# Inverting softmax denominators on 128 partitions by way of a small HBM tensor

## What is computed

```python
dots = jnp.einsum('bhid,bhjd->bhij', q, k) * d ** (-0.5)
dots = jnp.where(mask[None, None], mask_value, dots)
attn = jax.nn.softmax(dots, axis=-1)
out = jnp.einsum('bhij,bhjd->bhid', attn, v)
```

## Time and profile before

| | |
|---|---|
| three runs | 5416.88, 5419.1, 5422.39 us, median 5419.1 |
| profiled execution | span 5418.5 us from first to last instruction; no other time of it is given |
| TensorE (PE) busy | 5303.0 us, 98% |
| VectorE (DVE) busy | 3828.9 us, 71% |
| GpSimd (POOL) busy | 3028.9 us, 56% |
| ScalarE (ACT) busy | 2615.1 us, 48% |
| attention stage | about 727 to 2455 us |

### The profile page before, as it was taken

How to read it: one execution, slowest core, us unless ns; L and a number is a source line. 1 busy time by engine, 2 the same in 40 slices (tenths; PEclk the granted TensorE clock), 3 DMA queues, 4 the chain that set the end, 5 groups by cost and what they waited for, 6 DMA issues and landing times. The chain is left out here.

```text
span 5418.5 us, 102292 instructions
## 1 busy us (share of the span) xinstructions
PE 5303.0 (98%) x32880; PEld 4440.9 (82%) x32880; DVE 3828.9 (71%) x7311; ACT 2615.1 (48%) x3833; POOL 3028.9 (56%) x2716
## 2 busy tenths in 40 slices
PE   8999989999999999998999999999999999999999
PEld 6888866766666667667999999989999999999786
DVE  6666667778787877775676666766667666666664
ACT  3333333333343333335666666666666666666410
POOL 1222215666666665115777777777777777777514
PEclk9999989999999999998999999999999999999999
DMA  7777764444454444435676677767787676676748
GB/s 239 248 242 255 250 173 129 133 134 119 136 148 135 119 141 118 134 98 119 134 158 112 134 170 150 163 132 167 158 227 158 135 164 129 134 156 113 178 154 289
DMA packets 500414, 864.75 MB, mean 160 GB/s; under 512 B 64388, under 2 KB 165493, under 8 KB 497694
## 3 DMA queue, kind: packets, MB, share of 16 engines
q1 hardware_dynamic: 356014, 567.12, 33.2%
q0 software_dynamic: 140928, 292.13, 29.5%
q10 hardware_dynamic: 3312, 3.47, 0.3%
HBM read 498.49 MB, written 330.47 MB: 153 GB/s over the span
## 5 line engine op out<-in xcount | busy, mean ns | idle before, releaser
L1754 POOL DMA_INDIRECT mid_base<-e_rows,e_ox x556 | 1160.3, 2087 | 372.5 <-POOL e_ox L1749 239.5
L1865 DVE TENSOR_TENSOR e_wgu_lo<-e_wgu,e_wgu_hi 128x2048 fp32r<-128x2048 f32 x278 | 637.5, 2293 | 806.4 <-ACT e_wgu_hi L1788 676.6
L1742 POOL DMA_INDIRECT e_xg<-mid_xn,e_ix x556 | 625.5, 1125 | 336.4 <-POOL e_ix L1739 226.4
L1801 ACT CAST e_xT_hi<-e_ps_t 128x512 fp32r<-128x512 f32 x556 | 299.1, 590 | 929.8 <-PE e_ps_t L1931 929.8
L1069 POOL DMA_INDIRECT mid_ids<-b_pairs,b_cell x512 | 614.3, 1200 | 141.8 <-issue 141.0
L1944 PE MATMUL e_ps_g<-e_xT_hi,e_wgu_hi 128*128 128x256 f32 x2224 | 652.9, 294 | 1.7 <-issue 1.7
L1944 PE MATMUL e_ps_g<-e_xT_lo,e_wgu_hi 128*128 128x256 f32 x2224 | 630.0, 283 | 0.0
L1944 PE MATMUL e_ps_g<-e_xT_hi,e_wgu_lo 128*128 128x256 f32 x2224 | 629.7, 283 | 0.0
L1944 PE MATMUL e_ps_u<-e_xT_hi,e_wgu_hi 128*128 128x256 f32 x2224 | 629.4, 283 | 0.0
L1944 PE MATMUL e_ps_u<-e_xT_lo,e_wgu_hi 128*128 128x256 f32 x2224 | 629.4, 283 | 0.0
L1944 PE MATMUL e_ps_u<-e_xT_hi,e_wgu_lo 128*128 128x256 f32 x2224 | 629.4, 283 | 0.0
(11 more groups left out here) (286 smaller groups left out, 13368.0 us busy)
## 6 DMA issues: line engine op xcount, KB each, us to landing
b_xT_hi<-mid_xT_hi SPq DMA_DIRECT2D x32, 1024.0 KB
b_xT_lo<-mid_xT_lo SPq DMA_DIRECT2D x32, 1024.0 KB
mid_base<-b_x SPq DMA_DIRECT2D x32, 1024.0 KB
e_wgu<-in_gate_w SPq DMA_DIRECT2D x62, 512.0 KB
e_wgu<-in_up_w SPq DMA_DIRECT2D x62, 512.0 KB
e_wd<-in_down_w SPq DMA_DIRECT2D x62, 512.0 KB
ec_cell<-mid_base SPq DMA_DIRECT2D x88, 256.0 KB, 4.9
ab_q<-mid_q_hi SPq DMA_DIRECT2D x82, 256.0 KB, 4.0
```

What stands on the lines that cost most here:

```text
L1742: pool.indirect_dma_start(xg[s][:, i, :], None, t["xn"], bass.IndirectOffsetOnAxis(ap=ix[s][:, i:i + 1], axis=0))\
L1754: pool.indirect_dma_start(t[f"base{i}"], bass.IndirectOffsetOnAxis(ap=ox[s][:, i:i + 1], axis=0), rows[s][:, i, :], None, compute_op=ALU.a ...
L1801: act.copy(xT_hi[s][:, i * DC // 2 * RB:(i + 1) * DC // 2 * RB], ps_t[i][:, :]).then_inc(xT_hi_ready, 1)
L1865: dve.tensor_tensor(wgu_lo[s][:, :], wgu[s][:, :], wgu_hi[s][:, :].bitcast(F32), ALU.subtract)\
```

## The change

One of the 32 equal rows of each head's denominators is copied from `den` into a new tile `den16` of 128 partitions and 16 columns (`turn_den`), inverted there in one instruction (`invert`), stored to a new HBM tensor `rden` of 4 x 512 (`store_rden`), and loaded from there so that each of the four rows lands on 32 partitions of a new tile `rden` (`spread_rden`). `finish` multiplies by `rden` and waits for that load. The three transfers are issued by ScalarE, behind the exponents of slots 2, 5 and 7; the reciprocal stands in slot 4 of VectorE. The four reciprocals of 128 columns in slots 2 to 5 go.

```diff
@@ stage_b, tiles and semaphores @@
         den = sb("den", [P, QC])
+        den16 = sb("den16", [P, QC // DH])
+        rden = sb("rden", [P, QC])
...
-        rden_ready = sem("rden_ready")
+        den16_in = sem("den16_in")
+        den16_ready = sem("den16_ready")
+        rden_out = sem("rden_out")
+        rden_in = sem("rden_in")
@@ GpSimd @@
             def finish(u):
-                pool.wait_ge(rden_ready, QTC * (u + 1))
+                pool.wait_ge(rden_in, 16 * (u + 1))
                 pool.wait_ge(od_emptied, u + 1)
                 if u >= 2:
                     pool.wait_ge(att_out[u % 2], 16 * (u // 2))
-                pool.tensor_tensor(att[u % 2][:, :], o[:, :], den[:, :], ALU.mult).then_inc(att_ready, 1)
+                pool.tensor_tensor(att[u % 2][:, :], o[:, :], rden[:, :], ALU.mult).then_inc(att_ready, 1)
@@ ScalarE @@
+            def turn_den(u):
+                act.wait_ge(den_ready, u + 1)
+                act.dma_start(den16[:, :], den[0:P:DH, :].rearrange("h (j c) -> h j c", j=DH)).then_inc(den16_in, 16)
+
+            def store_rden(u):
+                act.wait_ge(den16_ready, u + 1)
+                act.dma_start(t["rden"].rearrange("h (j c) -> (h j) c", j=DH), den16[:, :]).then_inc(rden_out, 16)
+
+            def spread_rden(u):
+                act.wait_ge(rden_out, 16 * (u + 1))
+                if u:
+                    act.wait_ge(att_ready, u)
+                act.dma_start(rden[:, :], t["rden"][:, None, :].broadcast_to([HPC, DH, QC])).then_inc(rden_in, 16)
...
                     for kt, h in t_slots(n, k):
                         exponent(u, kt, h)
+                    if u and k == 2:
+                        turn_den(u - 1)
+                    if u and k == 5:
+                        store_rden(u - 1)
+                    if u and k == 7:
+                        spread_rden(u - 1)
...
+            turn_den(NU - 1)
+            store_rden(NU - 1)
+            spread_rden(NU - 1)
@@ VectorE @@
                 if u:
                     dve.wait_ge(att_ready, u)
+                    dve.wait_ge(den16_in, 16 * u)
                 dve.tensor_tensor(den[:, :], ps_d[:, :], p_null[:, :], ALU.add).then_inc(den_ready, 1)
...
-            def invert(u, i):
-                dve.wait_ge(den_ready, u + 1)
-                part = den[:, i * P:(i + 1) * P]
-                dve.reciprocal(part, part).then_inc(rden_ready, 1)
+            def invert(u):
+                dve.wait_ge(den16_in, 16 * (u + 1))
+                dve.reciprocal(den16[:, :], den16[:, :]).then_inc(den16_ready, 1)
...
-                    if 2 <= k < QTC + 2 and u:
-                        invert(u - 1, k - 2)
+                    if k == 4 and u:
+                        invert(u - 1)
...
-            for i in range(QTC):
-                invert(NU - 1, i)
+            invert(NU - 1)
@@ tensors in HBM @@
+        rden=d("rden", (HPC, QC))
```

More of the change, by code:

```diff
@@ L2322, in internal @@
         cnt=d("cnt", (P, EXPERTS)), ids=d("ids", (NSLOT, 2), I32), blk=d("blk", (1, 3 * P), I32), used=d("used", (1, 3), I32),
-        attT=d("attT", (DC, P, TOK)), passed=nc.alloc_semaphore("passed"))
+        attT=d("attT", (DC, P, TOK)), rden=d("rden", (HPC, QC)), passed=nc.alloc_semaphore("passed"))
 def layout(L0_attn_x, L0_attn_Wqkv, L0_attn_conv_w, L0_attn_conv_b, L0_attn_null_k, L0_attn_null_v, L0_attn_W_out,
```

## The result

The changed kernel takes 5638.71 us in the median, the kernel before 5417.99 in the runs beside it: a ratio of 1.0402 (95%: 1.0386 to 1.0419), so 221 us slower where 178 were forecast. One of the four runs of the changed kernel was disturbed (21823.6 us, clock 0.624 against 0.974); it counts in the median and is left out of the ratio. The profiled execution spans 5637.5 us, 219.0 more than before, and its mean granted clock is 0.974 instead of 0.992.

The account below looks back on a forecast made before the run. TensorE was taken to bound the attention stage. Stalls 45 (n = 1) and 99 (n = 3), clock 48, tail 6, less 20 for VectorE: +178 us on 5419 gives 5597 us, range 5508 to 5670.

Parts of the forecast that it names:

- the order on SP's queue: SP issues the next step's xT load behind the store of `att`, which waits for `finish`; slack 1.8 or 5.4 us.
- the late index scatters on GpSimd: Scatters behind `finish` come late by as much; with 3 us left before the mask's first reader, this costs nothing.
- The n = 1 stall: Query chunk 1: `finish` moves 4.6 us, xT slack is 1.8, TensorE stands 2.8 us; 16 x 2.8 = 45.
- The n = 3 stall: Query chunk 3: `finish` moves 12.0 us, xT slack is 5.4, TensorE stands 6.6 us; 15 x 6.6 = 99.
- The clock: TensorE at half clock after stalls: 2.1 us for each of 15 long and half of 16 short ones, 48 us.
- VectorE's gain: Fewer reciprocals shorten TensorE's row-maximum waits in the attention stage: 20 us taken, of at most 45.6.
- odd units cannot keep their share: Odd units lose their part of VectorE's gain, as TensorE only arrives earlier at the xT wait; 20 us taken.
- The tail: At the stage's end nothing covers the chain: 9.2 us against 3.38 for four reciprocals, 5.8 us more, once.
- (a): Rival: spread and move run on few DMA engines, stalls become 3.3 and 7.1 us; +211, 5630 us; chance 0.25.
- (b): Rival: short transfers, n = 1 stall under 1 us, only n = 3 pays; +97, 5516 us; chance 0.14.
- (c): Rival: xT loads still land in time, so only what VectorE gives back counts; -40, 5379 us; chance 0.04.
- (d): Rival: VectorE's wait for the move replaces the reciprocals, gain 0; 5617 us; chance 0.53 together with the main sum.

Follow-up runs that it names:

- experiment 1: Changed kernel, with SP issuing the xT loads ahead of the store of `att` in odd units instead of behind it: 5413.25 us, ratio 0.9989.
- experiment 3: Kernel before, with its four reciprocals four slots later (slots 6 to 9) and no new transfer: 5735.06 us, ratio 1.0585.
- experiment 6: Changed kernel, with the xT loads ahead of the store of `att`, and the reciprocal and its store both in slot 6: 5385.85 us, ratio 0.9934.
- experiment 4: Changed kernel, with the spreading load issued in slot 6 of ScalarE instead of slot 7: 5577.43 us, ratio 1.0288.
- experiment 5: Changed kernel, with the spreading load issued as four loads of 32 partitions, one for each head: 5594.34 us, ratio 1.0325.

## Why the prediction was right, and where its sizes were off

**The place was right.** The bound (TensorE's row-maximum wait, 45.6 us at most), the order on SP's queue, the 31 steps, longer stalls with n = 3 than with n = 1, a clock at 0.50 behind them: each stands in the rows after. Experiments 1 and 3 show that the xT load is the way by which the late `finish` costs time, in both directions. That the late index scatters on GpSimd cost nothing held too: with `finish` as late in experiments 1 and 6, the time does not rise above that of the kernel before.

**The n = 1 stall, 16 x 2.8 = 45, was 62.6.** The chain is not what failed: from the move's issue to `finish` it takes 10.61 us in the unit shown (2220.14 to 2230.75), 11.05 in my working. The reciprocal is where I put it (it hardly ever waits for the move, 3.5 us in the whole run, but for its place in VectorE's order); the store is followed by the spread's issue after 1.42 us instead of 2.1, and the spread takes 5.10 us to `finish` instead of 4.8. What failed is the step that took the xT load's own time as fixed and only moved its start. From its issue to the first matmul it takes 10.09 us (2232.46 to 2242.55), where my reading of the earlier trace rows left 8.1 (2062.02 to 2070.1). That is 2.0 more, less 0.4 of the chain, of the 1.8 us by which this stall (4.57) is longer than forecast. Over all 16 such steps the load takes 8.84 to 11.57 us to the first matmul, 9.46 in the median. The likely cause: SP issues three query loads at 2236.62 and the store of 1 MB of x at 2238.74, in the middle of it, which in the same unit before were issued only at 2070.66 and 2072.76, when xT was in. By an estimate 768 KB of queries at the 402 GB/s of the earlier trace rows are 1.9 us. The landings fit: in experiment 6, where SP issues nothing until the load has landed, these 16 loads land 7.74 to 10.47 us after their issue (median 8.00), here 8.80 to 11.53 (median 9.41). It was not tried by itself.

**The n = 3 stall, 15 x 6.6 = 99, was 125.8.** The place of the spread behind the exponent of slot 7 was right (experiment 4). In the unit shown the stall is 1.95 us longer than forecast: the issue comes 0.5 earlier, as it does not wait for that exponent's end; issue to `finish` is 0.2 shorter (4.64); the xT load takes 9.67 us to the first matmul (2178.32 to 2187.99), 1.1 more than the 8.6 that my working left (SP issues queries, keys and values behind it from 2179.43 on, before only from 2019.79 on); and `finish` takes 2.99 us, 1.7 more than 1.29. Together that is 2.1.

I had not seen that `finish`, moved later, would meet VectorE's adds. In the profiled execution after, 27 of the 64 multiplies start while an add of 128x2048 runs, and all of them end 1.13 to 1.25 us after the end of that add, however early they began; the other 37 take 1.26 to 1.30 us. In the unit shown the add ends at 2176.75 and the multiply at 2177.91. In the kernel before just one of 64 met such an add. So the two do not share: one stands until the other is done. The Trainium skill, page "SBUF — State Buffer", section "SBUF: two separate sides", says this of the ports that VectorE and GpSimd have in common: an exclusive lock for the whole instruction, which a VectorE instruction with two SBUF inputs holds against a GpSimd instruction that reads SBUF. The trace agrees.

**The clock, 48, was 62.** The price of one was right (2.1 us taken, 62 / 28 = 2.2 measured); 13 of the 16 short stalls had it and not half, as they were longer.

**VectorE's gain, 20, was about 38 by the remainder above; 43.2 is measured where nothing stands (experiment 6).** The step that failed is "odd units cannot keep their share". By units, with stalls and clock taken off, the changed kernel saves 9 us with n = 0, 12 with n = 2, 14 with n = 1 and 2 with n = 3, against 10.5, 11.0, 20.5 and nothing in experiment 6. So the units with n = 1 kept two thirds of their share, and those with n = 3 had none to lose. The step that leads from less work on VectorE to this gain is open too: experiment 3 has much of it with the old work in later slots.

**The tail, 6, was 3.0.** The chain there took 8.7 us from the move's issue to the multiply (2660.41 to 2669.15; worked out were 9.2), and the multiply starts 4.7 us later behind the denominators than before. Why only 3.0 of these reach TensorE was not followed.

With the terms after the fact the sum is 62.6 + 125.8 + 62 + 3 - 38 = 215, beside 219.0 in the span; the 4 left are the 3.6 that lie elsewhere. It closes because the 38 is the stage's remainder, so it proves nothing of that term. My sum was 41 too low, 44 of it in the stalls, 14 in the clock, and the gain and the tail took back 21.

**The rivals.** (a), few DMA engines, was real: experiment 5 and the share of 0.26 show it, and the rule of the Trainium skill that was cited for it (page "DMA: Bandwidth & Descriptors", section "Why a DMA increments its semaphore by 16 and not by 1"), by which four rows make four engines, agrees with the trace (0.26 of 16 engines is 4.2). Its 5630 us is nearest to the result, though partly by luck, since its bound on the transfers is about met by the spread alone, and what made up the rest, the longer xT load and the multiply beside the add, was in no rival. (b), short transfers, fell: the n = 1 stalls stayed. (c), loads in time, is what experiment 1 makes by hand; there it costs a new wait, and only experiment 6 comes near its 5379. (d), no gain on VectorE, fell in the kernel as given, where the row-maximum waits went. It is partly what experiment 1 shows: with the loads in time the wait for the move takes the place of the reciprocals in the n = 0 units.

Open stay the effect of the transfers issued behind the xT load; the clock's 62 us, which were counted and not isolated; and how much of VectorE's gain needs the shorter reciprocals and not just a later place for the old ones.

## What to carry to other kernels

Before a result is made later, look at what stands behind its store on the DMA queue: here a load that needed nothing of it waited, and moving that load was worth more than the edit. A short chain of small transfers wants spare slots at each link, since a transfer of 8 KB can wait for the megabytes issued before it, and a wait on a compute engine blocks all that is queued behind. The load that spreads four rows was better cut into several (44 us in experiment 5). And before work is taken off an engine that is not the bound, the same work in other slots is the simpler thing to try; that was left open here.

## What was not expected of the hardware

- An issue of a transfer on ScalarE does not wait for the exponent ahead of it to end: in the n = 3 unit the spread is issued at 2170.28, the exponent runs from 2170.20 to 2170.80. I had let each issue wait for the exponent's end, some 0.6 us.
- An 8 KB move took 6.2 us from issue to use behind the transfers that SP had issued before it (experiment 1), against the 2.0 us that I took.
- GpSimd's multiply stands until VectorE's large add has ended (2.99 us instead of 1.29), and the add until the multiply has (2.77 instead of 2.29).
